# Linear layers ahead of the attention: rows normalised in pairs, small tensors in PSUM, four base tiles moved into the first attention groups

## The chip, the cores and the metric

The kernel runs on one core of one Trainium2 chip. The metric is the device time of one launch in microseconds (us), the median of several runs. The program is one piece: batch 1 and batch 0 go through normalisation and the linear layers first, then 16 attention units follow (two batches of eight key/value heads).

## The reference

x is 2 x 1024 x 512. It is normalised row by row (no gain, no offset) to xn; the result is x plus an attention of xn plus a linear layer of xn with a routed low-rank part.

```python
xn = _layernorm(x, axis=-1)
x = x + attn(xn, ...) + ffn(xn, ...)

# attention: 32 query heads, 8 key/value heads of 128, weights of 4 bits with a scale per 128 rows
w = (qw.astype(float32) - 8) * repeat(scales, 128, axis=0)
q, k, v = xn @ w_q, xn @ w_k, xn @ w_v          # q and k with rotary tables
attn = softmax(causal(q @ k.T / sqrt(128))) @ v @ w_o

# linear part, 8 experts of rank 16, the two best for each row
probs = softmax(xn @ W_router.T)                 # 8 wide
topk_p, topk_i = top_k(probs, 2);  topk_p /= sum(topk_p)
combine = sum(one_hot(topk_i) * topk_p)
h = einsum('nd,erd->ner', xn, A_stack) * combine
out = xn @ W_base.T + b_base + einsum('ner,eor->no', h, B_stack) * 2.0
```

## The kernel before

Every matrix product is done in three products of high and low halves (`product`: high x high, high x low, low x high), so each float32 operand is split once: ScalarE (ACT) copies it to a `high` tensor of type fp32r, and VectorE (DVE) or GpSimd (POOL) subtracts that from the source into a `low` tensor. The product of a 128-row tile with 512 inputs is 12 matmuls.

TensorE's work is one list of steps, written by `tensor_order` and `unit`. The other engines have programs of their own; `behind(steps, us, kinds)` and `weights_due` place each of their operations at a step of that list by a model of lengths (`length`). The model only sets the order of the operations on each in-order engine; the real time is set by semaphores.

The linear stage runs over the batches in the order `STARTED = (1, 0)`; batch 1 is `PARKED` and its results are stored in DRAM until units 8 to 15. For each batch, by tiles of 128 rows (eight tiles):

- DVE takes the statistics of four tiles at once (`norm_stats`), ACT the root (`root`), DVE the reciprocal and a Newton step (`norm_scale`) and writes the normalised tile to `xn` (`normalise`, two buffers).
- TensorE transposes a tile (`turn_x`, four 128x128 transposes into one of three PSUM banks `turned`); ACT (`high`) and DVE (`low`) split it into `xnT_high` and `xnT_low`.
- `lora_a` multiplies the tile with 136 columns (A of all experts and the router, the part "ar" of the linear weights). `lora_read` on ACT copies it to SBUF. The list has turn_x 0, then turn_x t+1 ahead of lora_a t.
- Behind the eighth `lora_a`, `routing_logits`, `route_exps` (ACT) and `routing` (DVE) work out the two best experts and scale `hidden`. These are some thirty small operations, each waiting for the one before it (`own`). Their tensors `route`, `column`, `best`, `best_at`, `best_id` lie in SBUF.
- Meanwhile TensorE does `base` 0 to 3 (the tile with W_base, 12 matmuls of 512 columns), then `turn_hidden` 0 and 1 (transposes of `hidden`), `lora_b` 0 to 3 (3 matmuls each, added to the same PSUM place), then base and lora_b for tiles 4 to 7 in turn. `linear_read` on DVE adds the place to Y; POOL has added the bias (`add_bias`) before.

Products go to the four banks of `ring`: `ring_places` gives each step a place, `take_ring` waits until the place's last user has been read. The linear weights lie in what later holds `ctx_high` and `ctx_low`; their raw form lies in `probs`. ACT copies "ar" (544 wide), "b" (512) and "base" (2048), the last two right behind turn_x 1 of batch 1; DVE subtracts each (`linear_weight_low`).

Behind the linear stage come `project` for k, q0 and v of unit 0 (six times 12 matmuls), four `scores`, and the units. A unit has four heads and two halves, so eight groups, each with a pattern of letters: T transposes probabilities, V multiplies with the values, S computes scores of the next group, F a projection, O an output of a head pair, two tiles for each O. In unit 0 the first four groups have no outputs, as no unit is before it.

SP issues the loads and stores in its order: rows of batch 1 in three pieces, the identity, rows of batch 0 (`load_rows`), mask, rotary tables, the attention weights (two buffers; `load_weight` waits for POOL's split of the set before the last), `park_xn`, `park_y`. POOL scales and splits attention weights (`scale_weight`, `split_weight`: 0.6, 1.3, 0.6 and 1.3 us a set), adds biases and does part of the rotary work.

## Time and profile before

| | us |
|---|---|
| median of three runs | 2158.38 (2157.74 to 2159.29) |
| profiled execution | 2154.86 |
| its span | 2153.0 |
| PE (TensorE) busy | 2108.5 (98%) |
| DVE busy | 1514.3 (70%) |
| POOL busy | 1211.0 (56%) |
| ACT busy | 1014.4 (47%) |
| PE idle up to 250 us | about 28 |

PE, DVE, ACT, POOL and SP are the engines; PEld is TensorE's weight load. L985 is line 985 of the kernel. A page's busy time counts an instruction from its start to its end. `<-` behind a row names what ended the idle time before it. Matmul rows overlap: what counts is the distance between starts.

The linear stage of batch 1 runs from 11.4 to 74 us, that of batch 0 from 74 to 128 us; projections follow up to 144.6 us, and unit 0 begins there.

### The profile page before, as it was taken

The page shows a single profiled execution, that of the slowest core. Times are in us where ns is not written, and L with a number is a line of the kernel's source. Part 1 is how long each engine was busy: PE and PEld are TensorE (multiplying, and loading weights), DVE is VectorE, ACT ScalarE, POOL GpSimd, SP SyncE. Part 2 cuts the span into 40 slices and gives each one's busy share as a digit, 9 for nine tenths or more (in the row PEclk, how much of TensorE's full clock was granted, in tenths as well). Part 3 has the DMA queues.
Part 4 walks back from the last instruction along what each step waited for, and adds up shares of the span by engine and source line. Part 5 has one row for each costly group of instructions (what it writes and reads, how often), then busy time and mean ns, then how long its engine had stood idle before and what let it go on. Part 6 is the DMA issues. An engine that isn't in the chain of part 4 may idle for free.

```text
span 2153.0 us, 31030 instructions
## 1 busy us (share of the span) xinstructions
PE 2108.5 (98%) x11392; PEld 1804.8 (84%) x11392; DVE 1514.3 (70%) x3013; ACT 1014.4 (47%) x2193; POOL 1211.0 (56%) x1112
## 2 busy tenths in 40 slices
PE   7899999999999999999999999999999999999999
PEld 6778888888888888888888888888888888888887
DVE  5757677676767767676776767677676777767676
ACT  2225454454545445454544545454454545445453
POOL 2535666565656656565665656566555556556532
PEclk9999999999999999999999999999999999999999
DMA  7403232122222213222253422223232322322211
GB/s 240 130 6 69 65 59 70 45 64 54 70 55 59 68 45 66 54 70 55 57 145 66 125 53 70 54 57 62 50 69 53 71 55 57 60 52 69 45 40 55
DMA packets 169080, 145.84 MB, mean 68 GB/s; under 512 B 26336, under 2 KB 125408, under 8 KB 168416
## 3 DMA queue, kind: packets, MB, share of 16 engines
q1 hardware_dynamic: 165472, 137.80, 27.1%
q0 software_dynamic: 2112, 4.19, 0.6%
q8 instruction: 91, 1.49, 0.3%
q10 hardware_dynamic: 1344, 1.85, 0.2%
q14 instruction: 61, 0.50, 0.1%
HBM read 133.06 MB, written 10.75 MB: 67 GB/s over the span
## 4 chain that ended last, share of the span: by engine, by line
PE 93%; DVE 6%; ACT 1%; issue 0%; DMA 0%; SPq 0%; ACTq 0%
PE ring L985 44%; PE ring L1111 19%; PE O_ps L985 18%; PE turned L1122 11%; DVE rope L882 1%; DVE rope L881 1%; DVE rope L883 1%; DVE PT_low L813 1%; PE turned L1033 0%; PE turned L1092 0%; DMA Y<-in_x 0%; DVE probs L858 0%; ACT probs L688 0%; DVE stats L776 0%; DVE route L855 0%
## 5 line engine op out<-in xcount | busy, mean ns | idle before, releaser
L634 ACT ACTIVATE PT_high<-turned 128x512 fp32r<-128x512 f32 (+3 forms) x772 | 370.6, 489 | 587.9 <-PE turned L1122 559.7
L688 ACT ACTIVATE probs<-probs,negmax 128x128 f32<-128x128 f32 (+7 forms) x512 | 397.2, 776 | 263.2 <-DVE negmax L892 251.9
L813 DVE TENSOR_TENSOR PT_low<-turned,PT_high 128x512 fp32r<-128x512 f32 (+3 forms) x772 | 427.1, 555 | 95.0 <-ACT PT_high L634 85.8
L892 DVE CUSTOM_DVE_ANT_0 probs<-ring,mask_row 128x128 f32<-128x128 f32 (+7 forms) x512 | 383.8, 750 | 66.1 <-PE ring L1111 59.3
L1122 PE MATMUL turned<-ident,probs 128*128 128x128 f32 x2304 | 361.8, 274 | 3.4 <-ACT probs L688 3.4
L589 POOL TENSOR_TENSOR rope<-rope 128x512 f32<-128x512 f32 x160 | 206.5, 1291 | 266.3 <-DVE rope L883 265.2
L603 POOL TENSOR_TENSOR ctx_low<-ctx_f,ctx_high 128x512 fp32r<-128x512 f32 x128 | 165.2, 1291 | 274.6 <-ACT ctx_high L634 274.6
L1122 PEld LDWEIGHTS turned<-ident,probs 128*128 128x128 f32 x2304 | 277.3, 140 | 48.9 <-ACT probs L688 4.0
L985 PE MATMUL ring<-xnT_high,W_high 128*128 128x512 f32 x768 | 303.1, 395 | 0.0
L985 PE MATMUL ring<-xnT_low,W_high 128*128 128x512 f32 x768 | 300.0, 391 | 0.0
L985 PE MATMUL ring<-xnT_high,W_low 128*128 128x512 f32 x768 | 299.8, 390 | 0.0
L985 PE MATMUL O_ps<-PT_high,V_high 128*128 128x512 f32 (+3 forms) x768 | 286.5, 373 | 12.3 <-DVE PT_low L813 12.3
L597 POOL TENSOR_TENSOR Q_low<-rope,Q_high 128x512 fp32r<-128x512 f32 x128 | 165.2, 1291 | 211.1 <-ACT Q_high L634 210.8
L985 PE MATMUL O_ps<-PT_high,V_low 128*128 128x512 f32 (+3 forms) x768 | 266.5, 347 | 0.0
L985 PE MATMUL O_ps<-PT_low,V_high 128*128 128x512 f32 (+3 forms) x768 | 265.0, 345 | 0.0
L927 DVE TENSOR_TENSOR Y<-ring,Y 128x512 f32<-128x512 f32 x256 | 176.9, 691 | 118.1 <-PE ring L985 115.7
L881 DVE TENSOR_TENSOR rope<-ring,cos_sb 128x512 f32<-128x512 f32 x160 | 110.6, 691 | 211.0 <-PE ring L985 209.1
L1111 PE MATMUL ring<-K_high,Q_high 128*128 128x384 f32 (+5 forms) x768 | 246.5, 375 | 1.7
L1111 PE MATMUL ring<-K_high,Q_low 128*128 128x384 f32 (+5 forms) x768 | 221.7, 343 | 0.0
L1111 PE MATMUL ring<-K_low,Q_high 128*128 128x384 f32 (+5 forms) x768 | 220.7, 341 | 0.0
L551 POOL TENSOR_TENSOR scl<-raw,scl 128x512 f32<-128x512 f32 x160 | 206.7, 1292 | 13.3
L561 POOL TENSOR_TENSOR W_low<-scl,W_high 128x512 fp32r<-128x512 f32 x160 | 206.4, 1290 | 13.4
(96 smaller groups left out, 3635.6 us busy)
## 6 DMA issues: line engine op xcount, KB each, us to landing
R_sb<-row_sums SPq DMA_DIRECT2D x128, 256.0 KB, 4.2
raw<-in_qw_q SPq DMA_DIRECT2D x64, 256.0 KB, 4.7
scl<-in_scales_q SPq DMA_DIRECT2D x64, 256.0 KB, 8.6
raw<-in_qw_o SPq DMA_DIRECT2D x64, 256.0 KB, 4.2
scl<-in_scales_o SPq DMA_DIRECT2D x64, 256.0 KB, 4.5
raw<-in_qw_k SPq DMA_DIRECT2D x16, 256.0 KB, 4.3
scl<-in_scales_k SPq DMA_DIRECT2D x16, 256.0 KB, 5.7
raw<-in_qw_v SPq DMA_DIRECT2D x16, 256.0 KB, 4.8
```

The source lines that it names most:

```text
L551: own(nc.gpsimd.tensor_tensor(out=scl[:, n % 2, :], in0=as_float, in1=scl[:, n % 2, :], op=ALU.mult))
L561: nc.gpsimd.tensor_tensor(out=W_low[:, slot, :], in0=scl[:, n % 2, :], in1=W_high[:, slot, :].bitcast(f32), op=ALU.subtract).then_inc(w_do ...
L589: nc.gpsimd.tensor_tensor(out=rope_a[:, n % 2, :], in0=rope_a[:, n % 2, :], in1=rope_b[:, n % 2, :], op=ALU.add).then_inc(rope_sum, 1)
L597: nc.gpsimd.tensor_tensor(out=low[:, half(c)], in0=rope_a[:, n % 2, :], in1=high[:, half(c)].bitcast(f32), op=ALU.subtract).then_inc(rope_ ...
L634: return nc.scalar.activation(dst, src, ACT.Copy)
L688: nc.scalar.activation(probs[:, at], probs[:, at], ACT.Exp, bias=negmax[:, i:i + 1], scale=-1.0, accum_out=sums[:, i:i + 1]).then_inc(exp_ ...
L813: nc.vector.tensor_tensor(out=dst, in0=src, in1=high.bitcast(f32), op=ALU.subtract).then_inc(pt_low, 1)
L892: nc.vector.tensor_tensor_reduce(probs[:, prob_at[i]:prob_at[i] + n], score_place(u, h, i), mask_row[:, TOKENS - n:TOKENS], -1.0, -MASKED, ...
L927: nc.vector.tensor_tensor(out=Y[:, t, :], in0=place(step), in1=Y[:, t, :], op=ALU.add).then_inc(ring_read, 1)
L985: mm = nc.tensor.matmul(dst, lhs, rhs, start=start and n == 0, stop=stop and n == len(terms) - 1)
L1111: mm = nc.tensor.matmul(ps[:, lo:hi], lhs[:, tile], keys[:, lo:hi], start=first, stop=last)
L1122: mm = nc.tensor.transpose(turned_place(step)[:, q * P:(q + 1) * P], probs[:, at:at + P], ident[:, :])
```

## The change

- Rows: statistics, variance, root and scale of batch 1 are done for pairs of tiles (0,1), (2,3), (4,5), (6,7), each pair in the middle of the transposes of the pair before; batch 0 keeps fours. Tiles 0 and 1 are loaded by a DMA each. Rows of batch 0 and the rotary tables are loaded later.
- Weights: "ar" is copied by ACT ahead of the first root and subtracted by DVE ahead of the first scale. "base" is copied by ACT in four pieces behind turn_x 2 to 5 and subtracted in four pieces by POOL (`base_low`), which does that before all else. A new semaphore `base_done` counts them.
- Small tensors: `route`, `best_at`, `best_id`, `pair`, `share`, `var`, `root_var` and `newton` lie in the PSUM bank `O_ps`; `best`, `one_hot`, `total`, `rstd`, `stats` and `mv` stay in SBUF. Of the two tensor inputs of an operation at most one lies in PSUM.
- Order: turn_x 0 and 1 of batch 0 go ahead of base 7 of batch 1. base and lora_b of tiles 4 to 7 of batch 0 leave the linear stage and take the O letters of unit 0: tiles 4 and 5 in group 0, tile 6 in group 1, tile 7 in group 2. The biases of batch 0 move earlier on POOL.
- The model time of the first attention weights goes from 10 + 12.5 k to 24 + 8 k.

The diff without the parts that only rename:

```diff
+    if u == 0:
+
+        linear = [[("base", STARTED[1], t), ("lora_b", STARTED[1], t)] for t in range(4, NT)]
+        outputs[0:3] = [linear[0] + linear[1], linear[2], linear[3]]
...
+                if letter == "O" and of["O"] and of["O"][0][0] == "lora_b":
+                    steps.append(of["O"].pop(0))
...
-    steps = []
+    steps = [("turn_x", PARKED, 0), ("turn_x", PARKED, 1)]
     for b in STARTED:
-        steps += [("turn_x", b, 0)]
         for t in range(NT):
-            if t + 1 < NT:
-                steps.append(("turn_x", b, t + 1))
             steps.append(("lora_a", b, t))
+            if t + 2 < NT:
+                steps.append(("turn_x", b, t + 2))
 
         steps += [("base", b, t) for t in range(4)] + [("turn_hidden", b, 0), ("turn_hidden", b, 1)]
         steps += [("lora_b", b, t) for t in range(4)]
-        for t in range(4, NT):
-            steps += [("base", b, t), ("lora_b", b, t)]
+        if b == PARKED:
+            for t in range(4, NT):
+                if t == NT - 1:
+                    steps += [("turn_x", STARTED[1], 0), ("turn_x", STARTED[1], 1)]
+                steps += [("base", b, t), ("lora_b", b, t)]
...
-            t = 10.0 + 12.5 * k if u < 0 else began[u] + WEIGHT_SPAN * PREPARED.index(w) / len(PREPARED)
+            t = 24.0 + 8.0 * k if u < 0 else began[u] + WEIGHT_SPAN * PREPARED.index(w) / len(PREPARED)
...
-        LIN = {"ar": (0, KT * AR), "b": (KT * AR, HID), "base": (KT * AR + HID, KT * HID)}
+        LIN = {"ar": (0, KT * AR), "b": (TOKENS + HALF, HID), "base": (KT * HID, KT * HID)}
+        RAW = {"base": 0, "b": KT * HID, "ar": KT * HID + HID}
...
+        aside = O_ps[:, :]
+        route = aside[:, 0:3 * NT * NEXP].rearrange("p (a t e) -> p a t e", a=3, t=NT)
+        best_at, best_id = (aside[:, at:at + NT * 8].rearrange("p (t n) -> p t n", t=NT) for at in (256, 320))
+        best_at = best_at.bitcast(u32)
+        pair, share = (aside[:, at:at + NT] for at in (384, 392))
+        var, root_var, newton = (aside[:, at:at + NT] for at in (464, 472, 480))
...
+        def hidden_place(b, n):
+
+            if b == PARKED or n == 0:
+                places = PT_high[:, n, :], PT_low[:, n, :]
+            else:
+                places = lin_high[:, TOKENS:TOKENS + HALF], lin_low[:, TOKENS:TOKENS + HALF]
+            return [ap.rearrange("p (t n) -> p t n", t=4) for ap in places]
...
+            load_first(0, 1, first_loaded[0])
+            load_first(1, 2, first_loaded[1])
             sp.dma_start(ident[:, :], eye).then_inc(eye_loaded, 16)
-            load_x(PARKED, 1)
-            load_rows(0)
+            load_first(2, 4, y_loaded[0])
+            load_first(4, 6, first_loaded[2])
+            load_first(6, 8, y_loaded[1])
...
+                        load_rows(t // 4)
                         park_xn(t // 4)
...
+                        if t == 3:
+                            load_tables()
...
+            def base_low(k):
+                high, low, src = linear_weight("base", k)
+                if seen.new(lin_high_done, 3 + k):
+                    pool.wait_ge(lin_high_done, 3 + k)
+                nc.gpsimd.tensor_tensor(out=low, in0=src, in1=high.bitcast(f32), op=ALU.subtract).then_inc(base_done, 1)
...
+            for k in range(KT):
+                base_low(k)
...
+                    if b == PARKED:
+                        add_bias(b, t)
+                    elif t < 4:
+                        add_bias(b, t + 4)
+                for _, b, t in added[n]:
+                    if b != PARKED and t >= 4:
+                        add_bias(b, t - 4)
...
-            root(PARKED, 0)
             linear_weight_high("ar")
+            root(PARKED, 0, 2)
             for n in range(len(STEPS) + 1):
                 for s in turned_now[n]:
                     high(*s)
                     if s == ("turn_x", PARKED, 1):
-                        root(PARKED, 1)
+                        root(PARKED, 2, 4)
                         linear_weight_high("b")
-                        linear_weight_high("base")
+                    if s == ("turn_x", PARKED, 3):
+                        root(PARKED, 4, 6)
+                    if s == ("turn_x", PARKED, 5):
+                        root(PARKED, 6, 8)
+                    if s[:2] == ("turn_x", PARKED) and 2 <= s[2] < 2 + KT:
+                        linear_weight_high("base", s[2] - 2)
                     if s == ("turn_hidden", PARKED, 1):
-                        root(STARTED[1], 0)
-                        root(STARTED[1], 1)
+                        root(STARTED[1], 0, 4)
+                        root(STARTED[1], 4, 8)
...
+            def norm_var(b, lo, hi):
+                for t in range(lo, hi):
                     last = nc.vector.bn_aggr(mv[:, t, :], stats[:, t, :])
                 own(last)
-                nc.vector.tensor_scalar_add(var[:, cut], mv[:, cut, 1], EPS).then_inc(var_ready, 1)
-
-            def norm_scale(b, c):
-                n = 2 * nth(b) + c + 1
-                cut = slice(4 * c, 4 * c + 4)
+                nc.vector.tensor_scalar_add(var[:, lo:hi], mv[:, lo:hi, 1], EPS).then_inc(var_ready, 1)
+
+            def norm_scale(b, lo, hi):
+                n, cut = norm_number[b, lo, hi], slice(lo, hi)
                 if seen.new(sqrt_done, n):
                     dve.wait_ge(sqrt_done, n)
-                own(nc.vector.reciprocal(rstd[:, cut], rstd[:, cut]))
-
-                own(nc.vector.tensor_tensor(out=newton[:, cut], in0=rstd[:, cut], in1=rstd[:, cut], op=ALU.mult))
-                own(nc.vector.tensor_tensor(out=newton[:, cut], in0=newton[:, cut], in1=var[:, cut], op=ALU.mult))
-                own(nc.vector.tensor_scalar(newton[:, cut], newton[:, cut], -0.5, 1.5, ALU.mult, ALU.add))
-                own(nc.vector.tensor_tensor(out=rstd[:, cut], in0=rstd[:, cut], in1=newton[:, cut], op=ALU.mult))
+                r, w = rstd[:, cut], newton[:, cut]
+                own(nc.vector.reciprocal(r, root_var[:, cut]))
+
+                own(nc.vector.tensor_tensor(out=w, in0=var[:, cut], in1=r, op=ALU.mult))
+                own(nc.vector.tensor_tensor(out=w, in0=w, in1=r, op=ALU.mult))
+                own(nc.vector.tensor_scalar(w, w, -0.5, 1.5, ALU.mult, ALU.add))
+                own(nc.vector.tensor_tensor(out=r, in0=w, in1=r, op=ALU.mult))
+
+            def norm_rows(b, lo, hi):
+                for t in range(lo, hi):
+                    row_stats(b, t)
+                norm_var(b, lo, hi)
+                norm_scale(b, lo, hi)
...
+                own(nc.vector.tensor_reduce(pair, best[:, :, 0:2], op=ALU.add, axis=AX.X))
+                own(nc.vector.reciprocal(pair, pair))
                 for n in range(2):
-                    own(nc.vector.tensor_tensor(out=column[:, 1, :], in0=best[:, :, n], in1=column[:, 0, :],
-                                                op=ALU.mult))
-                    own(nc.vector.tensor_scalar(column[:, 1, :], column[:, 1, :], SCALING, None, ALU.mult))
-                    own(nc.vector.tensor_tensor(out=one_hot, in0=over_tiles(ids[:, :]),
+                    own(nc.vector.tensor_tensor(out=share, in0=best[:, :, n], in1=pair, op=ALU.mult))
+                    own(nc.vector.tensor_scalar(share, share, SCALING, None, ALU.mult))
+                    own(nc.vector.tensor_tensor(out=one_hot[:, :, :], in0=over_tiles(ids[:, :]),
                                                 in1=by_tile(best_id[:, :, n]), op=ALU.is_equal))
-                    dst = combine if n == 0 else one_hot
-                    own(nc.vector.tensor_tensor(out=dst, in0=one_hot, in1=by_tile(column[:, 1, :]), op=ALU.mult))
-                own(nc.vector.tensor_tensor(out=combine, in0=combine, in1=one_hot, op=ALU.add))
+                    dst = combine if n == 0 else one_hot[:, :, :]
+                    own(nc.vector.tensor_tensor(out=dst, in0=one_hot[:, :, :], in1=by_tile(share), op=ALU.mult))
+                own(nc.vector.tensor_tensor(out=combine, in0=combine, in1=one_hot[:, :, :], op=ALU.add))
...
-            norm_stats(PARKED, 0)
-            norm_scale(PARKED, 0)
+            row_stats(PARKED, 0)
+            row_stats(PARKED, 1)
+            norm_var(PARKED, 0, 2)
+            linear_weight_low("ar")
+            norm_scale(PARKED, 0, 2)
             normalise(PARKED, 0)
             normalise(PARKED, 1)
-            linear_weight_low("ar")
+            row_stats(PARKED, 2)
+            row_stats(PARKED, 3)
             turned_now, scored = behind(STEPS, 0.8, *TURNED), behind(STEPS, 0.1, "scores")
             summed, finished = behind(STEPS, 0.9, "turn"), behind(STEPS, 0.3, "values")
             others = behind(STEPS, 0.0, "project", "output", "lora_a", "lora_b")
             for n in range(len(STEPS) + 1):
                 for s in turned_now[n]:
                     low(*s)
-                    if s[0] == "turn_x" and s[2] + 2 < NT:
+                    if s == ("turn_x", PARKED, 1):
+                        norm_var(PARKED, 2, 4)
+                        norm_scale(PARKED, 2, 4)
+                        normalise(PARKED, 2)
+                        normalise(PARKED, 3)
+                    elif s == ("turn_x", PARKED, 2):
+                        row_stats(PARKED, 4)
+                        row_stats(PARKED, 5)
+                    elif s == ("turn_x", PARKED, 3):
+                        norm_var(PARKED, 4, 6)
+                        norm_scale(PARKED, 4, 6)
+                        normalise(PARKED, 4)
+                        normalise(PARKED, 5)
+                    elif s == ("turn_x", PARKED, 4):
+                        row_stats(PARKED, 6)
+                        row_stats(PARKED, 7)
+                    elif s == ("turn_x", PARKED, 5):
+                        norm_var(PARKED, 6, 8)
+                        norm_scale(PARKED, 6, 8)
+                        normalise(PARKED, 6)
+                        normalise(PARKED, 7)
+                    elif s == ("turn_x", PARKED, NT - 1):
+                        linear_weight_low("b")
+                        mask_rows()
+                    elif s[0] == "turn_x" and s[1] != PARKED and s[2] + 2 < NT:
                         normalise(s[1], s[2] + 2)
```

## Rows read from the trace of the kernel before

**Rows 1.** The page, first part: engine, busy us, share of the span, instructions.
```profile
PE 2108.5 (98%) x11392; PEld 1804.8 (84%) x11392; DVE 1514.3 (70%) x3013; ACT 1014.4 (47%) x2193; POOL 1211.0 (56%) x1112
```
**Rows 2.** Waits of PE from 0 to 250 us: total us, times, longest.
```profile
PE turned L1033 <- DVE probs L800: 11.4, 1, 11.4
PE turned L1067 <- DVE probs L858: 6.3, 2, 6.1
PE ring L985 <- DVE xnT_low L813: 4.6, 3, 3.0
PE turned L1122 <- ACT probs L688: 3.4, 4, 2.0
PE ring L985 <- DVE PT_low L813: 1.5, 2, 1.0
PE O_ps L985 <- DVE PT_low L813: 1.1, 1, 1.1
```
**Rows 3.** Waits of PE from 250 us to the end.
```profile
PE O_ps L985 <- DVE PT_low L813: 11.2, 19, 0.8
```
**Rows 4.** Stretches: length, busy us (instructions) by engine, granted clock, DMA share, GB/s.
```profile
23.90:42.40 18.50, 18.48 (x88) 18.48 (x89) 5.66 (x11) 3.81 (x9) 7.20 (x7) 1.00 0.87 279
57.23:74.07 16.84, 16.84 (x73) 13.63 (x73) 13.59 (x38) 1.42 (x3) 6.76 (x6) 1.00 0.46 149
76.14:89.72 13.58, 13.46 (x121) 13.32 (x121) 8.14 (x13) 5.57 (x13) 3.85 (x4) 1.00 0.67 201
89.72:101.08 11.36, 11.36 (x50) 8.90 (x49) 9.65 (x37) 1.82 (x3) 10.31 (x10) 1.00 0.28 88
101.08:107.19 6.11, 0.00 (x0) 0.00 (x0) 5.88 (x6) 0.00 (x0) 5.94 (x6) 0.67 0.26 87
109.72:128.23 18.51, 18.51 (x73) 14.91 (x73) 5.43 (x8) 0.08 (x1) 0.00 (x0) 0.90 0.00 1
160.30:167.00 6.70, 6.70 (x32) 6.00 (x33) 2.67 (x10) 3.36 (x8) 3.33 (x4) 0.75 0.24 27
187.20:192.00 4.80, 4.80 (x31) 4.32 (x32) 3.10 (x9) 3.07 (x8) 3.56 (x4) 1.00 0.04 2
```
**Rows 5.** Instructions at the start, by time: start, us, engine, what.
```profile
4.82 1.29 DVE L776 BATCH_NORM_STATS2 stats<-Y 128x6 f32<-128x512 f32 x2 [4.82 <-DMA Y<-in_x]
9.49 0.20 ACT L656 ACTIVATE rstd<-var 128x4 f32<-128x4 f32 x1 [5.09 <-DVE var L781]
9.60 0.64 ACT L634 ACTIVATE ctx_high<-probs 128x544 fp32r<-128x544 f32 x1
10.73 1.00 DVE L800 TENSOR_SCALAR probs<-Y,mv,rstd 128x512 f32<-128x512 f32 x2
11.43 1.94 PE L1033 MATMUL turned<-ident,probs 128*128 128x128 f32 x8 [11.43 <-DVE probs L800]
```
**Rows 6.** Routing of both batches, and POOL beside that of batch 0.
```profile
42.95 1.28 ACT L671 ACT_TABLE_LOAD   x1
42.97 0.22 DVE L820 TENSOR_REDUCE column<-probs 128x8 f32<-128x64 f32 x1 [3.46 <-ACT probs L634]
48.53 0.23 DVE L855 TENSOR_TENSOR route<-route,column 128x64 f32<-128x64 f32 x1
94.46 1.28 DVE L845 CAST best_id<-best_at 128x64 f32<-128x64 uint32 x1
103.58 5.91 POOL L582 TENSOR_TENSOR Y<-Y,R_sb 128x512 f32<-128x512 f32 x4
104.95 2.18 DVE L858 TENSOR_TENSOR probs<-probs,route 128x1024 f32<-128x1024 f32 x1
108.97 0.69 DVE L813 TENSOR_TENSOR PT_low<-turned,PT_high 128x512 fp32r<-128x512 f32 x1 [1.84 <-ACT PT_high L634]
```
**Rows 7.** Batch 0: a normalising and the POOL operation beside it.
```profile
80.71 1.27 POOL L561 TENSOR_TENSOR W_low<-scl,W_high 128x512 fp32r<-128x512 f32 x1
81.18 1.09 DVE L800 TENSOR_SCALAR probs<-probs,mv,rstd 128x512 f32<-128x512 f32 x1
```

135 lines of the change are left out of this document (59 added, 76 removed).

## The prediction

> **What bounds the kernel now.** I read the page's first part, then PE's waits before and behind 250 us, then the stretches between those waits, then single instructions around each. PE is busy 98% of the span [rows 1]: a gain can only come from its idle time, from its clock or from fewer products. Its waits are almost all in the first 250 us: 11.4 us before its first transpose, 6.3 us for the routing (6.1 of it in batch 0), 4.6 us in the lora_a loops, 3.4 us for exponentials, 1.5 and 1.1 us for splits [rows 2]. In the 1,900 us behind them it waits 11.2 us, in 19 pieces of at most 0.8 [rows 3], and the change touches nothing there. So everything is decided by 250 us.
>
> The clock costs too. In batch 1's lora_a loop 88 products take 18.50 us, 210 ns each; in batch 0's loop the same kinds take 13.58 us for 121, 112 ns each [rows 4]. That is the ratio of the two levels, 1.2 and 2.4 GHz (the clock column prints 1.00 for both; it has no record that early, so I go by the durations). PE had waited 11.4 us before the first loop, and was busy all through it without the rate rising. Behind the 6.11 us stretch with no product the granted clock is 0.90 over the next 18.51 us, for 73 instructions that took 16.84 us in batch 1 at 1.00. Behind the 2.0 us wait in unit 0 it is 0.75: 32 products in 6.70 us, against 31 in 4.80 [rows 2, 4].
>
> **The change part by part.** PE's products: the same set in another order. I find no edit that drops a product, though the short description says "no products of zeros"; I count it at nothing and expect 11392 PE instructions as before.
>
> *Start.* Before, PE's first transpose (11.43) follows the normalising (10.73), that the square root (ends 9.69), that the statistics of four tiles, the last of which waits for the second load [rows 5]. After, two tiles of 256 KB each are loaded apart and are enough. The first 512 KB had landed at 4.82 [rows 5], so tile 1 should be there by about 4.7; two statistics (1.29) and two small operations of about 0.2 end at 5.9. Then DVE splits "ar" ahead of the scale: its load lands at about 5.4, ACT's copy takes 0.64 [rows 5], DVE's subtraction about 0.7, so it ends at 6.8. The square root comes behind that copy on ACT. If the copy makes the program load another table first, its own table load of 1.28 [rows 6] stands between them and the root ends at 7.5; otherwise at 6.3 it is hidden. From the root's end to normalising is 1.04 us (9.69 to 10.73) [rows 5]. That gives 7.8 without and 8.6 with the table load: 2.9 or 2.1 us gained, and I take 2.5 (1.7 to 3.2, as the identity's landing near 8 us may hold PE). The Trainium skill, "ScalarE: Activation LUTs", section "What ACT_TABLE_LOAD costs", gives a switch of table 2.66 us with its drain; by that the gain would be 0.7 with the load, and the sum below 1.8 less. The row of 1.28 is followed by its exponential at once, so I use it.
>
> *Batch 1's loop.* It loses the 3.0 us wait behind ACT's and DVE's 2048-wide base copies [rows 2], which become four ACT copies of 0.6 and four POOL subtractions of 1.29. It gains waits for normalising in pairs. Worked in PE's order (four transposes 0.85 and twelve products 2.56 at the low rate): turn_x 2 follows lora_a 0, but the pair 2,3 gets its variance only behind low 1; turn_x 4 needs low 3, variance 0.4, root 0.3, four small operations and reciprocal 1.0, normalise 0.54, about 3.6 us after turn_x 3 ends, against 2.6 us of lora_a 2; turn_x 6 likewise. I get 0.6 + 1.2 + 1.2 = 3.0 us of waits, as many as go. On top, ACT issues base copies 1 and 3 right behind the roots for 4,5 and 6,7, so POOL's subtraction begins 0.75 us after the root and normalise 1.05 us after it. Normalising takes SBUF to SBUF, and beside a POOL operation one took 1.09 in place of 0.54, ending 0.3 behind POOL's [rows 7]. Then normalise 4 and 6 end 0.75 later each: 1.5 us lost (0 to 2). With 0.1 for the rest, the loop loses 1.6 us (3.3 to 0). The Trainium skill, "SBUF — State Buffer", section "SBUF: two separate sides", says that the pair of ports shared by VectorE and GpSimd is held for a whole instruction and the loser waits for all of it; by that each normalise ends 1.0 later and the loop loses 2.1.
>
> *Routing, batch 0.* The chain runs from the last lora_a to `hidden`. Before, small operations between SBUF tensors stretch to 1.2 or 1.3 us while POOL works (a cast of 64 elements 1.28, the last multiply 2.18 beside POOL's biases), but a subtraction that reads PSUM keeps its 0.69 beside the same biases [rows 6]. After, each of the two-input operations, the casts and the scalings has a PSUM operand. Without POOL beside it the first part took 42.97 to 48.76, 5.8 us [rows 6]; the second expert's four operations cost 0.9 as the first's did, the sum 0.26, the multiply of 1024 elements 1.2 (under twice the 0.69 for 512) [rows 6]: 8.2 us. It begins 0.5 us behind the last lora_a, so it ends at 8.7. PE's cover, base 0 to 3, is the 11.36 us to the empty stretch [rows 4]. So the 6.1 us go, and the next thing late is the wait for the split of the transposed `hidden`, 0.6 us before, 1.0 in batch 1 [rows 2]. The eight transposes then run at the high rate: 1.94 us for eight at the low one [rows 5], so 1.0 less, of which the later split takes back 0.5. The lower clock behind the gap cost 18.51 - 16.84 = 1.7. Together 6.1 + 0.5 + 1.7 = 8.3. No row shows DVE writing PSUM. Below nothing I exclude (8 to 512 elements cost the fixed 0.16 in any case); above, at twice the price for each of some 20 operations of 0.2, the chain is 4 us longer and PE waits 1.4. I take the price of reading PSUM. Batch 1's routing kept PE waiting 6.3 - 6.1 = 0.2 us [rows 2]; they go.
>
> *Between the batches.* turn_x 0 and 1 of batch 0 move ahead of base 7 of batch 1; what PE waited for their split (about 1.0 of the two waits of 1.6 in all) [rows 2] is covered by 2.8 us of base 7. Their rows are normalised behind the read of tile 4, so they are there. Gain 1.0. POOL's weight work and four biases now lie beside batch 0's normalising; a lock of 0.75 against a slack of 0.75 in each step (lora_a 1.3, normalise 0.54): I take a loss of 0.3 (0 to 1.5).
>
> *Unit 0.* Sixty products, 14 us, move from ahead of `project` into three groups that had no outputs. Their cost is the same there; what counts is the waits they cover. Group 0 gets 7 us ahead of its last `values`: the 2.0 us wait for the last exponential goes, and with it the clock's 1.7 us. Group 2 gets 3.5 us ahead of its last two: the 1.1 us wait for a split and one of the three waits of 0.5 go. Group 1 gets its tile in the middle, before its last scores, so the wait of 0.5 at its end stays. Gain 2.0 + 1.7 + 1.1 + 0.5 = 5.3 (3 to 5.8). DVE reads four tiles more there (0.69 each), in a stage like the later ones, where 16 `add`s a unit cost PE nothing [rows 3].
>
> *Queues.* SP: rows of batch 0 behind the first transposes, the tables behind the first park; needed 30 and 35 us later. load_rows(1) now waits for POOL's base parts, and behind it are only parking and weights. POOL stands in base_low until about 30 us, ahead of the weights, which PE now wants at about 100 instead of 128 us; six sets of 3.8 us and biases fit. Cost 0. If that cover were gone, PE would wait 3.8 us for each late set.
>
> **Sum:** 2.5 - 1.6 + 0.2 + 1.0 - 0.3 + 8.3 + 5.3 = 15.4 us. The profiled execution took 2154.9 (span 2153.0), so it would be 2139.5; the median is 3.5 above it, so 2158.4 - 15.4 = 2143.0.
>
> **The rivals.** (a) The forecast, 2138 to 2149: 0.73. (b) Small tensors in PSUM are no cure (a higher price there, or the operations still meet POOL): for it, no row shows such writes; against it, reads keep their 0.69. The 8.3 stay: 2151.3. Chance 0.09. (c) The moved products cover nothing: each holds a place of the four of `ring` until DVE's read, scores in pairs wait for it, and waits turn up elsewhere. The 5.3 go and some 2 more: 2150 to 2152. Against it, later units do the same with outputs. 0.08. (d) The other side: in batch 0's loop a wait lets the clock fall. Batch 1's loop shows that it does not rise again among these short products. Then eight tiles cost 3.33 in place of 1.75 us (+12.6), base 0 behind them 1.3 as in batch 1, and the wait that began it 3: 15.4 becomes -1.5, 2160; with a lock in each step 2163. It decides from a wait of about 2 us in the loop, as that in unit 0; POOL's biases beside normalising could make one. 0.05, a little over half of it beyond 0.2%. (e) The clock rises in batch 1's loop, since the start is another: 13 us more, 2130. Against it, 21 busy us without a rise. 0.04. (f) Products are dropped after all: 0.01, below 2140.
>
> **How the numbers follow.** 2143.0 is the likeliest case. The range 2138 to 2151.5 takes in (a), (b) and most of (c). Within 0.2% (4.3 us, about what can be told from no change) lie part of (d) and bad sums of (b) with (c): 0.05. Slower: 0.03. Faster: 0.92.
>
> **What the profile will show.** Right: the first transpose at 8.4 to 9.4 us; batch 1's loop still at 210 ns a product, with waits for normalise at tiles 2, 4, 6; no idle PE ahead of turn_hidden in batch 0 and no stretch below 1.00 there; small routing operations at 0.2 us throughout; POOL subtractions beside normalise at about 1.1; in unit 0 waits of 0.5 only. Wrong: PE waiting for `base_done` or `w_done`, any low stretch between 60 and 150 us, or a first transpose behind 10 us. The likeliest error of size is the first loop, where several waits of 1 us interlock.

## The result and the profile after

The changed kernel takes 2138.07 us (median of four runs, 2137.07 to 2139.22), the kernel before beside it 2158.06 (2157.45 to 2159.29). The ratio is 0.9907, with a 95% interval of 0.989 to 0.9924: 0.9% faster, by 20.0 us of the medians. The forecast was 2143.0, the range 2138.0 to 2151.5; the time lies at its lower edge. In the two profiled executions the gain is smaller: 2154.86 before, 2137.30 after, 17.6 us.

The first part of the page of the changed kernel, with the span above it: engine, busy us, share of the span, instructions.

```profile
span 2135.5 us, 31056 instructions
PE 2102.2 (98%) x11392; PEld 1801.1 (84%) x11392; DVE 1505.7 (71%) x3024; ACT 1016.2 (48%) x2199; POOL 1214.5 (57%) x1116
```

PE runs the same 11392 instructions as in [rows 1], so no product was dropped. It is busy 6.3 us less all the same. Two stretches of the kernel before, with products at the low level, explain most of that (from:to, length, busy us and instructions of PE, PEld, DVE, ACT and POOL, granted clock, DMA share, GB/s):

```profile
103.10:113.40 10.30, 5.65 (x17) 4.48 (x18) 6.63 (x7) 1.19 (x2) 6.39 (x5) 0.50 0.16 52
161.20:164.70 3.50, 3.50 (x16) 3.23 (x15) 2.51 (x8) 2.52 (x7) 3.12 (x3) 0.52 0.02 1
```

Half of their 9.15 us of products, 4.6 us, would not be there at the high level.

PE's waits in the first 250 us of the changed kernel: total us, times, longest.

```profile
PE turned L1113 <- DVE probs L859: 12.1, 3, 8.6
PE ring L1063 <- DVE xnT_low L872: 2.1, 2, 1.6
PE ring L1063 <- DVE PT_low L872: 2.0, 2, 1.0
PE turned L1203 <- ACT probs L742: 0.9, 2, 0.5
PE O_ps L1063 <- DVE PT_low L872: 0.6, 1, 0.6
```

Against [rows 2], the first wait is 8.6 in place of 11.4, and two waits of 1.72 for normalising are new in the same row (8.64 + 2 x 1.72 = 12.1). The routing's row of 6.3 is gone. The 4.6 of the lora_a loops are 2.1, the exponentials' 3.4 are 0.9, the last row's 1.1 is 0.6. Only the row of the transposed `hidden` grew, from 1.5 to 2.0. Behind 250 us the waits are nearly what they were, 10.6 us in place of 11.2 [rows 3]:

```profile
PE O_ps L1063 <- DVE PT_low L872: 10.6, 18, 0.8
```

Stretches of the changed kernel, in the same columns. In this order they are batch 1's loop, batch 0's loop, its base 0 to 3, its transposes of `hidden`, and a piece of group 1 of unit 0.

```profile
8.64:41.48 32.84, 27.75 (x128) 26.87 (x129) 18.52 (x48) 9.86 (x23) 8.80 (x7) 1.00 0.58 209
73.53:87.36 13.83, 13.71 (x120) 13.39 (x121) 9.88 (x14) 5.58 (x13) 9.35 (x9) 1.00 0.54 170
87.36:98.32 10.96, 10.96 (x51) 9.02 (x50) 6.71 (x42) 1.77 (x3) 7.74 (x8) 1.00 0.51 135
98.32:100.33 2.01, 1.03 (x10) 0.80 (x8) 0.69 (x1) 1.09 (x2) 2.01 (x3) 1.00 0.00 0
139.90:144.67 4.77, 4.77 (x32) 4.30 (x32) 4.04 (x10) 3.21 (x8) 2.23 (x3) 1.00 0.02 1
```

The empty stretch of 6.11 us in [rows 4] has no counterpart: PE goes from base 3 straight to the transposes at 98.32. The stretches of 0.90 and 0.75 are gone as well, and from 44 us to the end the granted clock stays at 1.00.

From the starts of PE's instructions in both traces the whole gain can be laid out, us:

| stretch | before | after | gain | forecast |
|---|---|---|---|---|
| start to first transpose | 11.43 | 8.64 | 2.8 | 2.5 |
| batch 1's loop, to base 0 | 30.98 | 32.84 | -1.9 | -1.6 |
| batch 1, base 0 to 3, to `turn_hidden` | 12.75 | 12.08 | 0.7 | 0.2 |
| from there to lora_a 0 of batch 0 | 20.98 | 19.97 | 1.0 | 1.0 |
| batch 0's loop | 13.58 | 13.83 | -0.25 | -0.3 |
| base 0 to 3 and the wait for the routing | 17.47 | 10.96 | 6.5 | 6.1 |
| `turn_hidden` to `lora_b` | 2.53 | 2.01 | 0.5 | 0.5 |
| low clock behind the routing | | | 1.7 | 1.7 |
| unit 0 up to group 4 | | | 6.1 | 5.3 |
| all behind it | | | 0.3 | 0 |
| sum | | | 17.5 | 15.4 |

### The profile page after: what moved, and what is told of

Its sections match the earlier page's. It is cut to its first block, busy times and chain, and to the rows that moved or that the text cites. A ratio compares the mean times of both kernels' runs of the same rounds, so it can differ in the third digit from the quotient of the medians.

```text
span 2135.5 us, 31056 instructions
## 1 busy us (share of the span) xinstructions
PE 2102.2 (98%) x11392; PEld 1801.1 (84%) x11392; DVE 1505.7 (71%) x3024; ACT 1016.2 (48%) x2199; POOL 1214.5 (57%) x1116
## 4 chain that ended last, share of the span: by engine, by line
PE 94%; DVE 5%; issue 0%; DMA 0%; ACT 0%; SPq 0%; DVEq 0%
PE ring L1063 44%; PE ring L1192 19%; PE O_ps L1063 19%; PE turned L1203 11%; DVE rope L940 1%; DVE rope L939 1%; DVE rope L941 1%; DVE PT_low L872 1%; PE turned L1113 0%; DMA Y<-in_x 0%; PE turned L1173 0%; DVE stats L828 0%; DVE probs L859 0%; DVE xnT_low L872 0%; DVE Y L925 0%
## 5 line engine op out<-in xcount | busy, mean ns | idle before, releaser
L1063 PE MATMUL O_ps<-PT_high,V_high 128*128 128x512 f32 (+3 forms) x768 | 286.3, 373 | 11.2 <-DVE PT_low L872 11.2
```

The costliest lines, as they stand in the source:

```text
L1063: mm = nc.tensor.matmul(dst, lhs, rhs, start=start and n == 0, stop=stop and n == len(terms) - 1)
```

## The experiments

The runs test the place of the small tensors, the moved products and both loops. No run takes the new start or the new order between the batches alone, so their gains of 2.8 and 1.0 us are read from the two traces. My theory after this comparison: the steps are right, the routing's 8 us come from the place of the small tensors alone, unit 0's 5 from the moved products alone, and the first loop can still be made shorter. What the traces left open was how far the median moves with the same kernel, whether POOL's new order did part of the routing's work, and what a fall of the clock in batch 0's loop would cost.

**The kernel before, again.** Unchanged, to see its spread.

> The kernel before, unchanged, profiled once more. Question: the medians moved 20.0 us (2158.1 to 2138.1) but the two profiled executions only 17.5 (spans 2153.0 and 2135.5). Theory A: executions of one kernel differ because the clock's low stretches come out longer or shorter (in the profiled one: up to 45.1 us, 10.2 us behind the routing, 3.4 us in unit 0), so repeats spread over some 3 us, the ratio to itself is 1.000 within 0.0015, and a second trace with another time shows the difference in low stretches ahead of 250 us. Theory B: the traces are undisturbed and the spread comes from elsewhere: the low stretches are the same to 0.5 us, and the difference lies behind 250 us or in DMA.

2155.89 us, ratio 0.9999 (0.999 to 1.0007). All 23 runs of the kernel before beside it lie between 2154.07 and 2160.66, median 2156.0. Its new trace has a longer low stretch behind the routing: 13.7 us here, 10.3 in the first trace. One PE wait (total, times, longest) and the stretch:

```profile
PE turned L1067 <- DVE probs L858: 7.0, 1, 7.0
```
```profile
102.70:116.40 13.70, 8.34 (x23) 6.55 (x24) 8.69 (x10) 1.19 (x2) 5.87 (x5) 0.51 0.14 40
```

The wait for the routing is 7.0 where it was 6.1 [rows 2], and the low level lasts 3.4 us longer, with 2.7 us more of products in it (8.34 against 5.65), half of which, 1.3 us, is lost. So the loss at the gap that the change takes away differs by some 2.2 us between two executions. But the whole span is only 0.6 us longer (2153.6 against 2153.0), as other stretches were shorter: batch 0's loop began 0.6 us earlier, for one. So it is not shown that this gap makes the spread of the kernel before.

The clock in unit 0 differs too. In this trace it stays at 1.00 behind the wait of 1.96 us for exponentials (at 161.7 us) and falls from 188.0 to 191.4 us, behind a wait of 1.06 us at 186.0.

**Small tensors in PSUM alone.** The kernel before with the routing's tensors in the bank `O_ps`; of the two tensor inputs of an operation one at most lies there. For that the sum of the two best became a `tensor_reduce`, as in the changed kernel; all else is as before.

```diff
+        # route, best_at, best_id, pair, share: views of O_ps
+        # total, one_hot: new tensors in SBUF
```

> One part alone: the kernel before with route, best_at, best_id and the small columns of the routing in the PSUM bank O_ps; POOL's biases and weights stay where they were, beside the routing of batch 0. Theory (placement): no operation of the chain has two SBUF inputs or takes SBUF to SBUF any more, so all cost 0.2 us, the chain takes 8.2 us instead of 16.9, PE's wait of 6.1 us ahead of the hidden transposes is 0, no low stretch follows: 8.3 us less, 2149.8 beside 2158.1. Rival (timing): it was POOL's work being elsewhere in the changed kernel that freed the chain; then the operations still stretch to 1.2 us here and the time stays within 2 us of before.

2147.49 us, ratio 0.9961 (0.9948 to 0.9974): 8.5 us less, against 8.3 expected. Three rows of its trace: start, us, engine, line, what.

```profile
94.56 3.79 POOL L585 TENSOR_TENSOR Y<-Y,R_sb 128x512 f32<-128x512 f32 x3
94.92 0.23 DVE L848 CAST O_ps<-O_ps 128x64 f32<-128x64 uint32 x1
97.78 1.22 DVE L860 TENSOR_TENSOR probs<-probs,O_ps 128x1024 f32<-128x1024 f32 x1
```

The cast of 64 elements that took 1.28 us beside POOL, and the last multiply that took 2.18 [rows 6], take 0.23 and 1.22 here, with POOL at work for 3.79 us beside the cast. PE has no wait for the routing any more: the chain ends at 99.00, and the transposes begin at 101.37, right behind base 3. So the add that became a reduce does not decide it: at its old 1.19 us the chain would still end ahead of base 3. Rival (b), that PSUM is no cure, falls: place shortens the chain, POOL's work being the same.

**Small tensors back in SBUF.** The other way round, in the changed kernel: normalisation's and routing's small tensors in SBUF, all the rest as after.

```diff
-        aside = O_ps[:, :]
+        aside = sb("aside", [P, 488])[:, :]
```

> The changed kernel with the whole aside tensor (routing's and normalisation's small tensors) in SBUF instead of PSUM, nothing else. If placement alone decides: 6.1 us of waiting and the low clock come back, about 8 us more, 2146. If POOL's new order does half the work: beside the chain (87.9 to 96.2 us) POOL is busy to 92.2 and from 95.2, so of the operations that met POOL before only the cast, the first subtraction and the multiply by combine would stretch, the chain would take 10 to 12 us against 10.9 us of cover: 0 to 2 us more, 2138 to 2140. I hold the second for likelier.

The median is 2152.71 us, ratio 0.9962 (0.9943 to 0.9981), but this median stands for neither of two groups of executions: five at 2138.61 to 2139.77 and seven at 2152.63 to 2154.92. The profiled one belongs to the first. There the routing does not keep PE waiting at all, as against 6.1 us before. The cast, POOL's next operation behind 94.86 us, and PE's transposes of `hidden`:

```profile
95.63 0.20 DVE L904 CAST aside<-aside 128x64 f32<-128x64 uint32 x1
98.72 1.39 POOL L589 TENSOR_SCALAR raw<-raw 128x512 f32<-128x512 int32 x1 [3.86 <-DMA scl<-in_scales_q]
100.98 1.03 PE L1148 MATMUL turned<-ident,probs 128*128 128x128 f32 x8
```

POOL stands idle from 94.86 to 98.72 us, waiting for a load, and the small operations from the cast on run in that gap in 0.2 us each, though they lie in SBUF; the last multiply takes 1.22. The chain ends at 99.63, ahead of base 3. So in this kernel the place in PSUM gives the routing nothing, and POOL's new order alone takes the 6.1 us away; in the kernel before the place alone gave 8.5. Either repair is enough. This group lies about 1 us above the changed kernel in the medians, and 2.5 us in the two traces. Of these, 1.1 us are in batch 1's loop and 0.6 in the wait ahead of batch 0's. In batch 1's loop, in the chains ahead of transposes 4 and 6, one operation on two elements meets a subtraction of POOL, and PE waits 2.28 us at each in place of 1.72.

```profile
22.38 1.26 DVE L845 TENSOR_SCALAR aside<-aside 128x2 f32<-128x2 f32 x1
```

The second group, 14 us slower, was unexpected, and the same kernel was profiled once more for it. In all seven of its executions the mean granted clock is 0.993 or 0.994, in the five of the first group 1.00.

> The changed kernel with its small tensors in SBUF once more, for the trace of an execution of the second group (2152.6 to 2154.9, 7 of 12). Theory: the clock falls to the low level at the start of batch 0's loop or in it, and does not rise before base 0: products of the loop at 210 ns, twelve more us there, and a low stretch in the clock's record between 75 and 105 us. Rival: the routing of batch 0 is late in that group (a wait of PE ahead of the hidden transposes and the low clock behind it, 8 us). If the execution is of the first group (2139), nothing is told.

2154.26 us: the second group. Two operations of POOL and two of DVE ahead of batch 0's loop, and PE's wait behind them (start, us, engine, line, what, idle time before and what ended it):

```profile
65.34 1.29 POOL L590 TENSOR_TENSOR scl<-raw,scl 128x512 f32<-128x512 f32 x1
65.36 1.28 DVE L834 TENSOR_SCALAR aside<-mv 128x4 f32<-128x4 f32 x1
68.67 1.28 POOL L600 TENSOR_TENSOR W_low<-scl,W_high 128x512 fp32r<-128x512 f32 x1
68.83 1.14 DVE L846 TENSOR_TENSOR rstd<-aside,rstd 128x4 f32<-128x4 f32 x1
78.24 0.33 PE L1063 MATMUL ring<-ctx_high,xnT_high 128*128 128x136 f32 x1 [2.48 <-DVE xnT_low L872]
```

The two DVE operations of four elements end with the POOL operations beside them. Two more between them took 0.88 and 0.55 us; in the first group's trace only one of this chain is stretched, to 1.15. The chain from L834 to L846 takes 4.6 us here and 2.4 there. DVE is late for the split of batch 0's first tile, and PE waits 2.48 us ahead of its lora_a 0. In the first group that wait is 1.0, in the changed kernel 0.4 and in its second trace 0.8. The stretch behind it (columns as above):

```profile
78.70:103.20 24.50, 24.50 (x119) 24.50 (x119) 7.95 (x13) 5.58 (x13) 17.30 (x16) 0.50 0.51 154
```

The granted clock is 0.50, the level of 1.2 GHz, from 78.7 to 106.0 us, though PE is fully busy. The loop takes 24.96 us (78.24 to 103.20), against 14.10 in the first group (75.93 to 90.03) and 13.83 in the changed kernel. For comparison the greater part of the same loop in the first group:

```profile
77.33:90.03 12.70, 12.59 (x111) 12.03 (x110) 8.75 (x12) 5.57 (x13) 9.36 (x9) 1.00 0.58 163
```

This is rival (d), seen on the chip: a wait of 2.5 us ahead of this loop, then a loop at half speed. The two traces of this kernel differ by 14.5 us, 10.9 of them in the loop and 1.5 in the wait. The forecast had put its point at about 2 us and its price at 12.6 us for the loop and 1.3 behind it. No run has a wait between 1.0 and 2.0 us at this place, so how near the changed kernel stands to the fall is not shown.

**Tiles 4 to 7 back ahead of the projections.** The changed kernel without the moved products.

```diff
-    if u == 0:
-        linear = ...; outputs[0:3] = ...
...
-        if b == PARKED:
+        if True:
             for t in range(4, NT):
```

> The changed kernel with base and lora_b of tiles 4 to 7 of batch 0 back ahead of project, where they were before; unit 0 has no outputs again. Theory: the waits of unit 0 come back: 2.0 us for the last exponential, 1.1 us for a split, 0.5 us, and 1.7 us of low clock behind the first: 5.3 us more, 2143.4. Measured from the hidden transposes to group 4 the part gave 6.0 us in the profiled executions, so up to 2144. Rival: the tiles cost in unit 0 what they save (places of the ring held up): within 1 us of the changed kernel.

2142.78 us, ratio 0.994 (0.9927 to 0.9953): 4.7 us above the changed kernel, 5.3 expected. PE's waits of [rows 2] in unit 0 are back: 3.4 us for exponentials (0.9 in the changed kernel) and 1.7 for splits (0.6). The two longest, and the low stretch behind them:

```profile
149.45 1.53 PE L1199 MATMUL turned<-ident,probs 128*128 128x128 f32 x12 [1.97 <-ACT probs L738]
173.71 0.33 PE L1059 MATMUL O_ps<-PT_high,V_high 128*128 128x128 f32 x1 [1.07 <-DVE PT_low L868]
175.40:178.80 3.40, 3.40 (x17) 3.35 (x16) 2.22 (x7) 2.70 (x6) 3.01 (x3) 0.53 0.02 1
```

The clock falls here behind the wait of 1.07 us and a shorter one that follows it, not behind that of 1.97. So it did in the second trace of the kernel before and in the kernel with PSUM alone; only in the first trace of the kernel before did it fall behind the 2.0. The moved products cover both waits, so the 1.7 us of the clock go either way. Rival (c), that the moved products cover nothing, falls.

**The changed kernel, again.** Unchanged, since the second group of the SBUF kernel raised the question whether this one has such a group too.

> The changed kernel, unchanged, on the chip and in the call of the next three, which are held against it. Expected 2138, span about 2136, and the same trace: first transpose at 8.6 us, waits of 1.7 us ahead of turn_x 4 and 6, clock low up to 44 us and nowhere behind. The variant with its small tensors in SBUF fell into two groups, 2138.6 to 2139.8 and 2152.6 to 2154.9. If the changed kernel also has such a second group, some of these runs come near 2152; if its shorter waits ahead of batch 0's loop (1.6 and 0.4 us against 1.9 and 1.0) keep it off, none does. I expect none.

2137.81 us (2136.55 to 2138.11), ratio 0.9911 (0.9894 to 0.9928), beside 2156.06 for the kernel before: 18.3 us. No run lies 14 us higher.

**Pairs earlier.** In batch 1's loop DVE takes the statistics, variance and scale of pairs (4,5) and (6,7) one transpose earlier than in the changed kernel, ACT their roots too, and ACT's base copies come behind them.

```diff
-                    if s == ("turn_x", PARKED, 3):      # root(4, 6); ACT
+                    if s == ("turn_x", PARKED, 2):
...
-                    if s == ("turn_x", PARKED, 5):      # root(6, 8); ACT
+                    if s == ("turn_x", PARKED, 4):
...
-                    elif s == ("turn_x", PARKED, 3):    # scale of 4, 5; DVE
+                    elif s == ("turn_x", PARKED, 2):
...
-                    elif s == ("turn_x", PARKED, 5):    # scale of 6, 7; DVE
+                    elif s == ("turn_x", PARKED, 4):
```

> The changed kernel with the normalisation of the pairs (4,5) and (6,7) of batch 1 one tile earlier on DVE and ACT, and ACT's base copies behind turn_x 3, 5, 6, 7, away from the roots. Theory: the two waits of 1.7 us ahead of turn_x 4 and 6 come from the chain split, variance, root, scale, normalise behind turn_x 3 and 5; they go, the loop ends 3.4 us earlier, at 38.1 in place of 41.5 us: 2134.7. Rival: DVE then splits tiles 2 to 4 later and the wait only moves to lora_a (gain under 1 us).

2134.04 us (2133.87 to 2134.63), ratio 0.9896 (0.9879 to 0.9913): 3.8 us below the changed kernel beside it, 3.4 expected. PE's waits on normalising before 250 us:

```profile
PE turned L1113 <- DVE probs L859: 8.7, 1, 8.7
```

Of 12.1 us in three waits the start's alone is left. The first normalising of each pair still takes 1.44 and 1.51 us beside POOL in place of 0.55, but PE does not wait for it.

**Raising the clock ahead of batch 1.** Products of 512 columns, thrown away, stand ahead of the first transpose, where PE is idle; once in the changed kernel, once with the earlier pairs.

```diff
+            for n in range(WARM):                       # 24
+                nc.tensor.matmul(ring[:, RING - 1, :], K_low[:, 0:P], K_low[:, 0:HALF], start=True, stop=True)
```

> The changed kernel with 24 products of 512 columns of constants ahead of the first transpose, into a ring bank that nothing uses until lora_a 3; their result is thrown away. They fit in the 8.6 us in which PE waits. Theory: batch 1's loop runs at half rate only because the clock was low when it began; started at the high level it stays there, as batch 0's loop does. A tile then costs 1.75 in place of 3.33 us, but the chain of normalising by pairs (6.6 us a pair) takes over: the loop ends at 31 to 34 us instead of 41.5, base 0 loses no 1.2 us: 8 to 11 us less, 2127 to 2130. Rival 1: the waits and the short products let the clock fall again in the loop: 0 to 3 us less, and executions that differ by 10 us. Rival 2: the loop's rate isn't the clock's: 210 ns a product as before.

> Both of the edits before: pairs normalised one tile earlier, and the 24 products ahead of the first transpose. Theory: with the clock high and the chain by pairs shortened, batch 1's loop is bound by DVE (0.69 split, 0.54 normalise, 0.7 statistics and 0.9 of small operations a tile, 2.8 us) and ends at 28 to 31 us: 11 to 14 us below the changed kernel, 2124 to 2127. Rival: DVE is late for everything at once and the clock falls: no better than the better of the two single edits.

2137.36 us and 2134.05 us: nothing gained against 2137.81 and 2134.04 without the products. Two stretches of the first of these kernels, and the instruction between them:

```profile
5.20:12.00 6.80, 4.64 (x24) 3.46 (x22) 5.13 (x15) 2.63 (x5) 0.00 (x0) 0.99 1.03 353
12.00:46.10 34.10, 30.18 (x131) 28.78 (x132) 19.10 (x70) 10.45 (x24) 8.80 (x7) 0.50 0.59 207
```
```profile
12.47 0.48 PE L1066 MATMUL ring<-ctx_high,xnT_high 128*128 128x136 f32 x1 [2.63 <-DVE xnT_low L875]
```

The clock rose, and fell again within PE's wait of 2.63 us for the split of tile 0. With the pairs earlier that wait was 2.3 us, and the clock fell behind it too. The next runs fill this wait.

**Filling the waits of batch 1's loop.** Both changes, 22 products ahead, and further thrown-away products ahead of each lora_a of batch 1: ten before the first, three before each of the next six.

```diff
+                if b == PARKED:
+                    for n in range(FILL[t]):
+                        nc.tensor.matmul(place(step), K_low[:, 0:P], K_low[:, 0:HALF], start=True, stop=True)
```

> The kernel with both edits (pairs earlier, 22 products ahead), with more thrown-away products of 512 columns in batch 1's loop: 10 where PE waits for the split of tile 0, three ahead of each lora_a 1 to 6. Theory: in the traces of both kernels with products ahead the clock rose at 5.2 to 5.9 us and fell at 12.0 to 12.8, in PE's wait of 2.3 to 2.6 us for the split; with that wait filled it stays high, the loop is bound by DVE at 2.8 us a tile, base begins at about 34.5 instead of 37.7 us and loses no 1.2 us: 4 to 6 us below 2134, so 2128 to 2130. Rival: the short waits between the tiles let it fall all the same; then the filling costs 0.7 us to 1.3 us a tile at the low rate and the kernel is 5 to 9 us above 2134.

2140.26 us (2139.46 to 2141.48), ratio 0.9927 (0.9913 to 0.994). The loop itself did what it should, and batch 0 paid for it:

```profile
6.20:31.30 25.10, 23.61 (x168) 21.06 (x167) 20.58 (x57) 10.37 (x25) 5.76 (x5) 1.00 0.66 236
64.30:91.60 27.30, 27.30 (x127) 26.77 (x127) 9.97 (x19) 7.34 (x16) 14.52 (x14) 0.51 0.65 188
```
```profile
PE ring L1067 <- DVE xnT_low L876: 2.1, 1, 2.1
```

Base 0 of batch 1 begins at 31.3 us in place of 37.7 without the filling, so 6.4 us were won. But the last row, PE's waits between 55 and 70 us, shows that DVE is not ready for batch 0 that early: PE waits 2.1 us ahead of its loop, and the clock is at the low level for all of it. It is rival (d) once more, reached by PE being early, not by DVE being late.

**The same with statistics of tiles 2 and 3 behind the first splits.** To shorten the wait ahead of the first lora_a.

```diff
-            row_stats(PARKED, 2)
-            row_stats(PARKED, 3)
...
+                    if s == ("turn_x", PARKED, 0):
+                        row_stats(PARKED, 2)
+                    elif s == ("turn_x", PARKED, 1):
+                        row_stats(PARKED, 3)
```

> The same, and the statistics of tiles 2 and 3 of batch 1 behind the split of tiles 0 and 1 on DVE instead of ahead of it. Theory: DVE had waited there for the load (1.0 us in the changed kernel) and taken 1.4 us, ahead of the split that lora_a 0 waits for; lora_a 0 then begins 1.1 us earlier, and the end 1 us earlier than in the filled kernel. Rival: the chain for tiles 2 and 3 becomes that much later, and turn_x 2 waits instead: no gain.

2140.19 us, ratio 0.9925 (0.9911 to 0.9938): no gain. lora_a 0 starts at 11.99 in place of 12.55 us, 0.56 earlier where 1.1 was expected, and transpose 2 gives it back (PE's longest wait on normalising between 10 and 30 us, this kernel and the one before it):

```profile
PE turned L1118 <- DVE probs L863: 1.5, 1, 1.5
```
```profile
PE turned L1117 <- DVE probs L863: 1.2, 1, 1.2
```

Behind the wait of 1.5 us the clock was at the low level from 15.1 to 18.5 us, which it was not in the first filled kernel.

**Both loops filled.** The first of the filled kernels, with nine thrown-away products (in place of ten) ahead of the first lora_a of batch 1, and nine ahead of that of batch 0 too.

```diff
-FILL = (10, 3, 3, 3, 3, 3, 3, 0)
+FILL = (9, 3, 3, 3, 3, 3, 3, 0)
...
-                if b == PARKED:
+                if b == PARKED or t == 0:
```

> The filled kernel (22 products ahead, 9 where PE waits for tile 0's split, three ahead of lora_a 1 to 6 of batch 1), with 9 thrown-away products also ahead of lora_a 0 of batch 0. In the filled kernel without them batch 1's loop ran at the high level (base began at 31.3 in place of 37.7 us), but PE then waited 2.2 us ahead of batch 0's loop, the clock fell at 64.3 us and stayed low for 27.3: 2140.3. Theory: that wait was all it took; with it filled, batch 0's loop runs at 1.75 us a tile in place of 3.33 and base 0 behind it in full: 12.6 and 1.2 us less, 2126.5 (2125 to 2128.5), below both kernels of the case, with one clock record from 6 us to the end. Rival: the loop's short products alone let the clock fall: again 2140, with a fall between 65 and 75 us.

2128.58 us (2127.56 to 2131.66), ratio 0.9868 (0.9851 to 0.9884), where 2126.5 was expected and 2128.5 was the upper bound. It is the fastest kernel of the study, 9.5 us below the changed kernel's 2138.1 and 29 below the kernel before beside it (2157.74). Its stretches of both loops, and PE's waits for splits between 9 and 95 us:

```profile
6.20:31.30 25.10, 22.93 (x152) 20.38 (x150) 20.11 (x56) 10.04 (x24) 4.21 (x4) 0.93 0.66 238
60.00:90.00 30.00, 29.79 (x194) 26.78 (x193) 19.71 (x70) 8.50 (x19) 19.22 (x19) 1.00 0.62 197
```
```profile
PE ring L1067 <- DVE xnT_low L876: 0.8, 2, 0.5
```

The second stretch is the one that was at 0.51 before: with the wait of 2.1 us filled the clock stays. The first has 3.4 us at the low level (15.4 to 18.8), which costs 1.7 of the miss of 2.1 us. It stands behind a wait of 1.17 us for normalising; in the first filled kernel the same wait, as long, left the clock high.

## Why the prediction was right and where it was short

The gain was forecast as 15.4 us and came out at 20.0. The direction held, and each part moved the way that was forecast. What failed is the size of the sum, at two steps. The terms came to 17.5 us in the profiled executions: unit 0 gave 6.1 where 5.3 stood, batch 1's routing and base 0.7 where 0.2 stood, the routing 8.7 where 8.3 stood. And the last step, which carried a gain worked out on one profiled execution unchanged to the median, put at nothing a difference that measured 2.4 us; its cause stays open. One reading of cause was too narrow as well: for the routing the forecast counted on PSUM, where POOL's new order alone does the same. Part by part:

**Start: right, 0.3 small.** The forecast worked out 7.8 to 8.6 us for normalising, by whether a second table load would stand ahead of the root. It does. Instructions of the changed kernel by time (start, us, engine, what, idle time before and what ended it):

```profile
5.25 1.28 ACT L709 ACT_TABLE_LOAD   x1
6.55 0.16 ACT L709 ACTIVATE O_ps<-O_ps 128x2 f32<-128x2 f32 x1
8.64 1.97 PE L1113 MATMUL turned<-ident,probs 128*128 128x128 f32 x8 [8.64 <-DVE probs L859]
```

But it began at 5.25, right behind the copy of "ar", and ended at 6.53, before DVE's split of "ar" was over at 7.12. So the root was not last: the split was. Normalising began at 8.04 and the transpose at 8.64, 2.8 us earlier. The load takes 1.28 us and the root starts 0.02 behind it. The Trainium skill, "ScalarE: Activation LUTs", section "What ACT_TABLE_LOAD costs", adds a drain of 1.38 us to such a switch; this trace shows none, so the forecast did well to go by its row.

**Batch 1's loop: right in sign and size, wrong in its places.** -1.9 against -1.6. Still at the low rate, as foreseen, and rival (e), that the clock rises here, did not come about. The waits are not 0.6 + 1.2 + 1.2 but one ahead of lora_a 0 and one each at transposes 4 and 6:

```profile
10.05 1.42 DVE L828 BATCH_NORM_STATS2 stats<-Y 128x6 f32<-128x512 f32 x2 [1.01 <-DMA Y<-in_x]
12.25 0.48 PE L1063 MATMUL ring<-ctx_high,xnT_high 128*128 128x136 f32 x1 [1.65 <-DVE xnT_low L872]
22.00 1.26 POOL L607 TENSOR_TENSOR ctx_low<-probs,ctx_high 128x512 fp32r<-128x512 f32 x1 [3.40 <-ACT ctx_high L688]
22.43 1.57 DVE L859 TENSOR_SCALAR probs<-Y,mv,rstd 128x512 f32<-128x512 f32 x2
```

What the forecast missed is the first row: DVE has the statistics of tiles 2 and 3 in its program ahead of the first split, and they wait for a load until 10.05. lora_a 0 waits 1.65 us, and by the time transpose 2 is due its tile is there. Moving these statistics behind the split, in the filled kernel, brought lora_a 0 forward by 0.56 us, so as far as that run shows they are a part of that wait and not all of it. The lock is in the last two rows: two normalisings take 1.57 beside POOL in place of the 1.00 of [rows 5]. That is 0.57 for a pair, where the sum had 0.75. The Trainium skill, "SBUF — State Buffer", section "SBUF: two separate sides", has the loser of that port wait for the whole of the other's instruction. Here POOL's had 0.83 us left when DVE's row begins, and 0.57 was paid: a wait behind it, as the page says, but shorter than what was left. The experiment with earlier pairs puts the two waits at 3.8 us together.

**Routing: right.** The forecast had the chain at 8.2 us; it took 8.35 in batch 1 and 8.36 in batch 0. Two of its operations in batch 0:

```profile
92.15 0.23 DVE L904 CAST O_ps<-O_ps 128x64 f32<-128x64 uint32 x1
95.02 1.22 DVE L916 TENSOR_TENSOR probs<-probs,O_ps 128x1024 f32<-128x1024 f32 x1
```

Writing PSUM, for which no row was there, costs what reading it costs: 0.16 to 0.23 us for the small ones. With the clock this part gave 8.7 against 8.3, and PSUM alone in the kernel before gave 8.5. It is partly luck, though, that the term came out right: in the changed kernel the cause it named was not the only one at work. With the tensors in SBUF the new order of POOL's work takes away all of the routing's wait. What PSUM is needed for in the changed kernel is batch 1's loop (1.1 us) and the place ahead of batch 0's loop, where the wait stays at 0.4 to 0.8 us and the 14.5 us of rival (d) away. The forecast gave that rival 0.05 and named its cause as POOL beside normalising; it comes from POOL beside the small operations ahead of normalising.

**Batch 1's routing and base: 0.5 small.** 0.7 against 0.2. **Unit 0: 0.8 small.** 6.1 against 5.3. Both are in part for the same reason: a wait costs PE more than its row says. Instructions of PE in the kernel before, around its waits of 2.0 and 0.5 us for exponentials (start, us, line, what, idle time before and what ended it):

```profile
158.05 0.27 PE L985 MATMUL O_ps<-PT_high,V_low 128*128 128x128 f32 x1
160.29 2.02 PE L1122 MATMUL turned<-ident,probs 128*128 128x128 f32 x12 [1.96 <-ACT probs L688]
...
173.99 0.27 PE L985 MATMUL O_ps<-PT_high,V_low 128*128 128x128 f32 x1
174.73 0.66 PE L1122 MATMUL turned<-ident,probs 128*128 128x128 f32 x4 [0.46 <-ACT probs L688]
```

Such a product moves the next one by 0.11 us where PE waits for nothing (157.94 to 158.05). From 158.05 to the transposes it is 2.24, so the wait costs 2.13 and not 1.96; at the second one 0.63 and not 0.46. Each wait that goes gives 0.17 us more than its row, since a row counts from the modelled end of the product before. In unit 0 the exponentials' waits went from 3.4 to 0.9 us and the wait for a split from 1.1 to 0.6, 3.0 us in all, against the forecast's 3.6; with the clock's 1.7 and 0.17 for each of some four waits that is 5.4 of the 6.1. The other 0.7 has no row. Of batch 1's 0.7 the routing's wait of 0.15, counted so, is 0.3; for the rest I have no row. The routing of batch 0 has the same 0.17 in its 6.5, and about 0.2 by which base 0 to 3 ran faster.

**Between the batches and batch 0's loop: right to 0.1.** No stretch of POOL's weight work stops PE, and PE waits for no set of weights: the queues' cost of nothing holds.

**From the sum to the median: 2.4 us, the largest miss.** The steps gave 15.4, the traces 17.5: 2.1 us, spread over small terms. The medians moved by 20.0. The sum was made against a profiled execution of 2154.86 and carried unchanged to a median 3.5 above it. The kernel before, measured beside the changed one, has a median 3.2 above that execution, while the changed kernel's profiled execution stands only 0.8 below its median: a difference of 2.4 us that no trace shows. The second trace of the kernel before loses some 2.2 us more at the routing than the first, by a wait 0.9 longer and more products at the low level, but its span is only 0.6 us longer, so it does not explain the 2.4. In later comparisons the kernel before has medians between 2156.0 and 2157.7, and the changed kernel measured once more gains 18.3 us, so up to 1.7 of the 20.0 may belong to that comparison alone. How much is which I leave open. The time came within 0.1 us of the range's lower end, 2138.0: the range had no room for the distance between one profiled execution and the median.

## What to carry to other kernels

Look for the small operations of a chain that come out at the length of another engine's instruction beside them, and move one of their operands to PSUM, or the other engine's work elsewhere; one of the two was enough here. Ask then which other short chains the same tensors sit in, since the one ahead of a loop of short products can cost more than the one you meant. Count a wait together with what the clock does behind it: ahead of batch 0's loop a wait of 2.1 us cost a half-rate loop, one of 1.0 nothing. Don't take one trace's fall of the clock as fixed: in unit 0 it came behind one wait in one execution and behind another in the next. And when you make a sum against one profiled execution, let the range hold the distance between it and the median, as the part you remove may be the part that varies.
